# Expert results scaled per slot and added to the output by scattering transfers, in a graph transformer layer

## The chip, the cores and the metric

The kernel runs on one core of a Trainium2 chip. The metric is the device time of one execution in microseconds; of the kernel before there are three runs, with a median of 1598.75 (1598.35 to 1600.05). One further execution was profiled; all rows below are from it.

## The reference, cut to what matters

1250 tokens of width 1024 go through a layer norm, a graph convolution and a linear attention, both added to the input. The change is in the last stage, a mixture of 8 experts of which each token takes the best 2:

```python
x = x + _L0_gnn_ref(xn, edge_index, ...) + _L0_mix_ref(xn[None], ...)[0]
x = x + _L0_ffn_ref(_layernorm(x, axis=-1)[None], ...)[0]

def _L0_ffn_ref(x, gate_w, gate_b, expert_w, expert_b):
    logits = jnp.einsum('bsd,ed->bse', x, gate_w) + gate_b
    topv, topi = jax.lax.top_k(logits, K)          # K = 2 of E = 8
    keep = jax.nn.one_hot(topi, E).sum(axis=-2)
    gate_score = jax.nn.softmax(jnp.where(keep > 0, logits, -jnp.inf), axis=-1)
    expert_out = jnp.einsum('bsd,edo->bseo', x, expert_w) + expert_b
    return jnp.einsum('bseo,bse->bso', expert_out, gate_score)
```

## The kernel before

Five engines run their own instruction streams, written out by hand, and meet only at semaphores. Graph stage and attention are the first two thirds of the span. Then `x2`, the layer's value ahead of the experts, lies in SBUF as 10 tiles of 128 tokens (the last has 98), and its normalised rows in DRAM as `x2n_half[0]` and `x2n_half[1]`, 512 columns each.

*Routing* (VectorE, L1322 to L1413). For every token the two experts and the two gates. Tokens are counted per expert (two small products on TensorE, L1713), and each pair of token and expert gets a slot. An expert has whole tiles of 128 slots, at least two; here there are 23 tiles in all, of at most `MAXT` = 35. The table from slot to token, `slots`, comes from 20 products of one-hot matrices (`hotr`, `hott`, L1721). The gates `gab` are worked out at L1416 to L1424, behind that. `pos` holds the slot of each token's two results.

*Experts.* A tile T is handled so:
- POOL (`gather_tile`, L803 and L806) gathers the tokens' rows into `xg`, in two halves of 512 columns. Half c of tile T + 1 may come when TensorE has transposed that half of tile T.
- TensorE (`tile`) does for each half h four slabs k of the products (three matmul forms L1745, L1746 and L1748 for both column halves), and behind each half the four transpositions of that half of tile T + 1 (L1731). Behind the second half `prod_done` is signalled.
- ScalarE (L1043) and VectorE (L1380) take the transposed half out of PSUM as a high and a low part, `mth` and `mtl`.
- VectorE (`copy_out`, L1393) adds the expert's bias `ebb` to the products and writes `ybuf`. PSUM holds two tiles of products, `ybuf` one.
- SyncE (`store_tile`, L590) stores `ybuf` to the rows of that tile in `slot_y`, a tensor in DRAM of 35 x 128 rows. `slot_y` was filled with rows of `x` in the attention stage (L527), so that no row of it is undefined.

When the last tile of expert e has its products, SyncE issues the 8 slabs (512 KB each) of expert e + 2's weights (L545), and after the tile's store the bias of e + 1. ScalarE (`high`, L1010) and VectorE (L1408) split each slab of expert e + 1 in a high and a low part: slabs 0 to 3 and 4 to 7 behind the two halves of `prepare` for the next tile. Before, VectorE's `copy_out` of an expert's last tile comes behind all of these.

*The end.* Twenty gathers of POOL (L829), 512 KB each, fetch each token's two results from `slot_y`: ten for the first expert as soon as the experts before the last are stored, ten for the second when everything is stored; the last four of these wait for a buffer. VectorE multiplies each by its gate and adds it to `x2` (L1433), and SyncE stores each tile of `x2` to `out` (L615).

Of the kernel before, what the change touches and what calls it, by code (L numbers as in the profile page):

```python
# [24 lines left out]
FILL = MAXT * P // (KT - 1)  # L25
assert FILL * (KT - 1) == MAXT * P and FILL <= NP
# [29 lines left out]
def gps_layer(nc, x, dst_pairs, src_cols, dst_cols, wg, bg, wq, bq, wk, bk, wv, bv, wo, bo, orf,  # L56
              gate_w, gate_b, expert_w, expert_b, out):
    x2n_half = [nc.dram_tensor(f"x2n_half{c}", [NP, CW], F32, kind="Internal").ap() for c in range(NC)]
    slot_y = nc.dram_tensor("slot_y", [MAXT * P, D], F32, kind="Internal").ap()
# [4 lines left out]
    with ctx:  # L64
# [49 lines left out]
        hott = keep("hott", [P, 2 * TT, MAXT], F32, s1)  # L114
# [103 lines left out]
        pc = ExitStack()  # L218
        gathered = keep("gathered", [P, 2 * KT, D], F32, pc)
        pc.close()  # L220
# [32 lines left out]
        pos = keep("pos", [P, 2, TT], I32)  # L253
        token = keep("token", [P, TT], F32)
# [5 lines left out]
        here = keep("here", [P, NC], I32)  # L260
        gw = keep("gw", [P, KT, E], F32)
# [107 lines left out]
        s_pos = sem("s_pos")  # L369
        slot_hot = sem("slot_hot")  # L370
        slots_filled = sem("slots_filled")
# [12 lines left out]
        y_stored = [sem(f"y_stored{c}") for c in range(NC)]  # L384
        z_stored = [sem(f"z_stored{c}") for c in range(NC)]
        a_gathered = sem("a_gathered")
        b_gathered = [sem(f"b_gathered{i}") for i in range(TT // 2)]
        comb_a = sem("comb_a")
        comb_b = sem("comb_b")
# [59 lines left out]
        def _(sp):  # L449
# [72 lines left out]
            with sp.Fori(1, KT) as j:  # L522
                for i, w in enumerate((wk, wv, wq)):

                    sp.wait_ge(a_w, START + 3 * j + i)
                    sp.dma_start(hraw[:, :, :], w[ds(j, 1)].rearrange("a p k n -> (a p) k n")).then_inc(a_raw, 16)
                sp.dma_start(slot_y[ds((j - 1) * FILL, FILL), :], x[0:FILL, :]).then_inc(slots_filled, 16)  # L527

# [57 lines left out]
            def store_tile(T, e, last):  # L586
                for c in range(NC):

                    sp.wait_ge(y_copied[c], T + 3)
                    sp.dma_start(slot_y[ds(T * P, P), c * CW:(c + 1) * CW],  # L590
                                 ybuf[:, c, :]).then_inc((z_stored if last else y_stored)[c], 16)

            def expert(e, par, last):
                more, begin = tiles(sp, e)
                with sp.Fori(0, more) as i:
                    store_tile(tile_of(begin + i), e, last)
                T = tile_of(begin + more)
                if not (isinstance(e, int) and e >= E - 2):

                    sp.wait_ge(prod_done, T + 1)  # L600
                    load_expert(e + 2, par)
                store_tile(T, e, last)
                if not last:

                    load_bias(e + 1)

            sp.wait_ge(slots_filled, 16 * (KT - 1))
            sp.wait_ge(s_cnti, 1)
            experts(sp, expert)


            for t in range(TT):
                n = LAST if t == TT - 1 else P
                sp.wait_ge(comb_b, t + 1)
                sp.dma_start(out[t * P:t * P + n, :], x2[0:n, t, :]).then_inc(s_out, 16)  # L615
# [4 lines left out]
        def _(pool):  # L620
# [31 lines left out]
            for signal in (rest_taken, rest_over, a_w, t_done, s_done, sq_ready, phi_done, kv_done, aux_done, kv_evac,  # L652
                           mt_trans, *y_stored, *z_stored):
                pool.sem_inc(signal, START)
# [116 lines left out]
            g.iota(token[:, :], [[P, TT]], base=0, channel_multiplier=1,  # L771
# [51 lines left out]
            for c in range(NC):  # L823
                pool.wait_ge(y_stored[c], START + 16 * begin)
                apart(pool)

            def gather_results(t, i, at, done):
                n = LAST if t == TT - 1 else P
                g.indirect_dma_start(gathered[0:n, at, :], None, slot_y[:, :],  # L829
                                     bass.IndirectOffsetOnAxis(ap=pos[0:n, i, t:t + 1], axis=0)).then_inc(done, 16)  # L830

            for t in range(TT):
                gather_results(t, 0, t, a_gathered)

            pool.wait_ge(s_pos, 1)
            for c in range(NC):
                pool.wait_ge(z_stored[c], START + 16 + 16 * more)
                apart(pool)
            for t in range(TT):
                if t >= 6:  # L840

                    pool.wait_ge(comb_b, t - 5)
                gather_results(t, 1, TT + t % 6, b_gathered[t // 2])
# [3 lines left out]
        def _(act):  # L847
# [216 lines left out]
        def _(dve):  # L1064
# [271 lines left out]
            v.tensor_tensor(both[:, :, :], oneh[:, 0], oneh[:, 1], ALU.add).then_inc(s_both, 1)  # L1336
            dve.wait_ge(route_done, 1)
# [19 lines left out]
            v.tensor_copy(pos[:, :, :], posf[:, :, :]).then_inc(s_pos, 1)  # L1357
# [25 lines left out]
            def copy_out(T, e, i, begin, last):  # L1383
                for c in range(NC):
                    dve.wait_ge(prod_done, T + 1)
                    dve.wait_ge(eb_ready, 16 * (e + 1))

                    if last:
                        dve.wait_ge(y_stored[c], START + 16 * begin)
                        dve.wait_ge(z_stored[c], START + 16 * i)  # L1390
                    else:
                        dve.wait_ge(y_stored[c], START + 16 * T)
# [3 lines left out]
            def expert(e, par, last):  # L1396
                more, begin = tiles(dve, e)
                with dve.Fori(0, more) as i:
                    for h in range(2):
                        prepare(begin + i + 1, h)  # L1400
                    copy_out(begin + i, e, i, begin, last)
                for h in range(2):
                    prepare(begin + more + 1, h)
                    if not last:
# [5 lines left out]
                copy_out(begin + more, e, more, begin, last)  # L1410

            dve.wait_ge(route_done, 2)
            v.tensor_copy(slots[:, :], bank(2, MAXT)).then_inc(slots_ready, 1)  # L1413

            dve.wait_ge(s_ge, 1)
            link(v.tensor_scalar(gd[:, 3, :], gd[:, 1, :], 1.0, None, ALU.add))  # L1416
            link(v.reciprocal(gd[:, 2, :], gd[:, 3, :]))
            link(v.tensor_tensor(gd[:, 3, :], gd[:, 1, :], gd[:, 2, :], ALU.mult))
            link(v.tensor_tensor(sel[:, 0, :], one, two, ALU.is_lt))
            link(v.tensor_tensor(sel[:, 1, :], two, one, ALU.is_lt))  # L1420
            for i in range(2):
                link(v.tensor_tensor(gab[:, 1, i, :], sel[:, i, :], gd[:, 2, :], ALU.mult))
                link(v.tensor_tensor(gab[:, 2, i, :], sel[:, 1 - i, :], gd[:, 3, :], ALU.mult))
                link(v.tensor_tensor(gab[:, 0, i, :], gab[:, 1, i, :], gab[:, 2, i, :], ALU.add))  # L1424
# [5 lines left out]

            def combine(t, i, at, done):
                n = LAST if t == TT - 1 else P
                v.scalar_tensor_tensor(out=x2[0:n, t, :], in0=gathered[0:n, at, :], scalar=gab[0:n, 0, i, t:t + 1],  # L1433
                                       in1=x2[0:n, t, :], op0=ALU.mult, op1=ALU.add).then_inc(done, 1)

            dve.wait_ge(a_gathered, 16 * TT)
            for t in range(TT):
                combine(t, 0, t, comb_a)
            for t in range(TT):
                dve.wait_ge(comb_a, t + 1)  # L1440
                dve.wait_ge(b_gathered[t // 2], 32)
                combine(t, 1, TT + t % 6, comb_b)
# [3 lines left out]
        def _(pe):  # L1446
# [272 lines left out]
            for i in range(2 * TT):  # L1719
                n = LAST if i % TT == TT - 1 else P  # L1720
                ins = mm(bank(2, MAXT), hotr[0:n, i, :], hott[0:n, i, :], start=(i == 0), stop=(i == 2 * TT - 1))  # L1721
# [96 lines left out]
```

## Time and profile before

| | us |
|---|---|
| median of 3 runs | 1598.75 |
| the profiled execution | 1597.88 |
| its span | 1596.3 |
| TensorE busy in the span | 1410.3 |
| last products of the experts end | 1550.77 |
| stores of the output, first and last issue | 1573.47, 1592.8 |

The span is the time from the first to the last instruction, and the execution takes 1.6 us more. Times in rows count from the start of the span. "Idle before" in brackets is the time that the engine stood still ahead of a row, and what released it. Matmuls are pipelined and their ends modelled. PEclk is the clock granted to TensorE as a share of full speed: 1.00 is 2.4 GHz, 0.50 is 1.2 GHz. A row with "x4" merges four instructions that follow each other.

### The profile page before, as it was taken

How to read it: one execution, taken by the hardware profiler on the slowest of the kernel's cores; microseconds unless marked ns; L12 is line 12 of the kernel's file. 1: busy time of each engine (PE TensorE's matmuls, PEld its weight loads, DVE VectorE, ACT ScalarE, POOL GpSimd, SP SyncE). 2: the span in 40 equal slices, each digit the busy share in tenths (PEclk: the TensorE clock that was granted, in tenths of full speed). 3: DMA queues.
4: the chain of work that ended last, by engine and by line, in shares of the span. 5: the costliest groups of instructions: out<-in, count | busy, mean ns of one | idle time of the engine just before them, and what ended most of it. 6: DMA issues, size and time to landing. Idle time of an engine off the chain costs nothing.

```text
span 1596.3 us, 26325 instructions
## 1 busy us (share of the span) xinstructions
PE 1410.3 (88%) x8396; PEld 1243.6 (78%) x8460; DVE 763.6 (48%) x1492; ACT 466.1 (29%) x777; POOL 381.6 (24%) x380
## 2 busy tenths in 40 slices
PE   5787778978899999999999999997999499999980
PEld 2465566878889999999999999996888388888870
DVE  8755443414344444444444444445454435444536
ACT  7412132401123333333333333333123023223310
POOL 7421443233230101010101010003134211222133
PEclk9999999988899999999999999998999599999995
DMA  4110111244322020202020202004244326666558
GB/s 151 50 37 17 60 47 70 72 137 123 98 71 87 19 87 17 89 15 90 14 91 14 91 13 79 1 1 134 68 140 146 122 88 232 244 237 219 208 195 289
DMA packets 64532, 158.06 MB, mean 99 GB/s; under 512 B 7978, under 2 KB 28922, under 8 KB 64032
## 3 DMA queue, kind: packets, MB, share of 16 engines
q1 hardware_dynamic: 55200, 127.20, 22.5%
q0 software_dynamic: 9280, 30.17, 5.9%
q8 instruction: 32, 0.52, 0.1%
q14 instruction: 20, 0.16, 0.0%
HBM read 119.98 MB, written 55.71 MB: 110 GB/s over the span
## 4 chain that ended last, share of the span: by engine, by line
PE 76%; DMA 7%; DVE 6%; issue 5%; ACT 2%; POOL 2%; DVEq 2%; SPq 1%; POOLq 0%; ACTq 0%
PE PB L1568 7%; PE PB L1570 7%; PE PB L1569 7%; PE PB L1745 5%; PE PB L1746 5%; PE PB L1748 5%; PE PB L1604 5%; PE PB L1627 4%; PE PB L1470 4%; DMA y_scratch<-xrow 3%; PE PB L1552 2%; PE PB L1553 2%; PE PB L1554 2%; PE PB L1511 2%; PE PB L1512 2%
## 5 line engine op out<-in xcount | busy, mean ns | idle before, releaser
L1568 PE MATMUL PB<-xh,hw 128*128 128x416 f32 (+1 forms) x576 | 204.8, 356 | 0.0
L1570 PE MATMUL PB<-xh,hw 128*128 128x416 f32 (+1 forms) x576 | 203.1, 353 | 0.0
L1569 PE MATMUL PB<-xl,hw 128*128 128x416 f32 (+1 forms) x576 | 202.9, 352 | 0.0
L1745 PE MATMUL PB<-mwh,mth 128*128 128x512 f32 x368 | 149.2, 405 | 1.3 <-issue 1.3
L1470 PE MATMUL PB<-ohs,ohd 128*128 x471 | 106.9, 349 | 48.5 <-DVE ohs L1116 34.5
L1746 PE MATMUL PB<-mwl,mth 128*128 128x512 f32 x368 | 144.7, 393 | 0.0
L703 POOL CAST hw<-hraw 128x1024 fp32r<-128x1024 f32 x24 | 24.9, 1038 | 457.6 <-PE PB L1570 456.3
L1470 PEld LDWEIGHTS PB<-ohs,ohd 128*128 x534 | 52.0, 98 | 102.4 <-issue 84.6
L1748 PE MATMUL PB<-mwh,mtl 128*128 128x512 f32 x368 | 114.0, 391 | 0.0
L1114 DVE TENSOR_SCALAR ohd<-iota,dc 128x128 f16 x178 | 56.1, 315 | 114.5 <-PE PB L1470 103.3
L1569 PEld LDWEIGHTS PB<-xl,hw 128*128 128x128 f32 x576 | 108.7, 189 | 1.3
L1568 PEld LDWEIGHTS PB<-xh,hw 128*128 128x128 f32 x576 | 108.6, 189 | 1.3 <-issue 0.2
L1570 PEld LDWEIGHTS PB<-xh,hw 128*128 128x128 f32 x576 | 108.6, 189 | 1.2
L1539 PE MATMUL PB<-hh,AT 128*128 128x256 f32 x400 | 103.7, 298 | 5.9 <-DVE hr L1130 5.8
L1116 DVE TENSOR_SCALAR ohs<-iota,sc 128x1280 f16 x178 | 106.3, 597 | 0.0
L1540 PE MATMUL PB<-hr,AT 128*128 128x256 f32 x400 | 102.2, 294 | 0.0
L1043 ACT ACTIVATE mth<-PB 128x512 fp32r<-128x512 f32 x48 | 28.8, 599 | 231.3 <-PE PB L1731 215.6
L1380 DVE TENSOR_TENSOR mtl<-PB,mth 128x512 fp32r<-128x512 f32 x48 | 33.0, 688 | 131.0 <-ACT mth L1043 126.9
L1511 PE MATMUL PB<-wqh,xh 128*128 128x256 f32 x320 | 91.7, 286 | 3.2 <-DVE xl L1123 1.7
L955 ACT ACTIVATE qf<-PB,biasT 128x416 f32<-128x416 f32 (+1 forms) x48 | 29.2, 609 | 214.5 <-PE PB L1570 167.3
L1512 PE MATMUL PB<-wql,xh 128*128 128x256 f32 x320 | 90.5, 283 | 0.0
L1513 PE MATMUL PB<-wqh,xl 128*128 128x256 f32 x320 | 90.5, 283 | 0.0
(260 smaller groups left out, 3138.6 us busy)
## 6 DMA issues: line engine op xcount, KB each, us to landing
mraw<-expert_w SPq DMA_DIRECT2D x64, 512.0 KB, 5.2
slot_y<-x SPq DMA_DIRECT2D x7, 2560.0 KB, 11.6
slot_y<-ybuf SPq DMA_DIRECT2D x46, 256.0 KB, 3.3
count_rests<-ATf POOLq DMA_DIRECT2D x9, 640.0 KB, 3.3
xrow<-x SPq DMA_DIRECT2D x40, 128.0 KB, 2.4
y_scratch<-xrow SPq DMA_DIRECT2D x40, 128.0 KB, 2.4
yrow<-y_scratch SPq DMA_DIRECT2D x20, 256.0 KB, 2.9
x2n_half<-xhat SPq DMA_DIRECT2D x20, 256.0 KB, 2.5
```

The lines of the kernel that those rows point to most:

```text
L1116: v.tensor_scalar(ohs[:, ds(2 * side + p, 1), :].rearrange("p a n -> p (a n)"), iota[:, :], sc[:, ds(col, 1)], None, ALU.is_equal).then_in ...
L1470: ins = mm(PB[:, 1536 * s + c0:1536 * s + c0 + n], ohd[:, ds(2 * side + p, 1), :].rearrange("p a n -> p (a n)"), ohs[:, ds(2 * side + p, 1 ...
L1511: mm(o, xh[:, k, at], wqh[q % 2][:, k, :], start=(k == 0), stop=False)
L1512: mm(o, xh[:, k, at], wql[q % 2][:, k, :], start=False, stop=False)
L1539: mm(o, AT[:, b, at], hh[:, q % 2, b, :], start=(b == 0), stop=False)
L1540: ins = mm(o, AT[:, b, at], hr[:, q % 2, b, :], start=False, stop=(b == TT - 1))
L1568: mm(bank(i, n), hw[:, wi, 0, k, :], xh[:, k, c0:c0 + n], start=(k == 0), stop=False)
L1569: mm(bank(i, n), hw[:, wi, 0, k, :], xl[:, k, c0:c0 + n], start=False, stop=False)
L1570: ins = mm(bank(i, n), hw[:, wi, 1, k, :], xh[:, k, c0:c0 + n], start=False, stop=(k == KT - 1))
L1745: mm(y[c], mth[:, k, :], mwh[par][:, k, c * CW:(c + 1) * CW], start=(k == 0), stop=False)
L1746: mm(y[c], mth[:, k, :], mwl[par][:, k, c * CW:(c + 1) * CW], start=False, stop=False)
L1748: ins = mm(y[c], mtl[:, k, :], mwh[par][:, k, c * CW:(c + 1) * CW], start=False, stop=(k == KT - 1))
```

## The change

`slot_y`, its fills and stores, the twenty gathers, `pos` and the combination are gone. The output rows get `x2` first, by ten stores that SyncE issues directly after the load of expert 1. Each slot's gate and output row come out of the routing products: `hott` has two values per slot, the token and the gate, 70 columns instead of 35, so the gates are worked out earlier, ahead of the wait for the counts. Empty slots get row 4096, which the transfer leaves out as out of bounds. ScalarE multiplies `ybuf` by the gates of its slots (`scale`), and POOL adds the tile's 128 rows to `out` with one indirect transfer that adds (`add_tile`), waits until it has landed, and signals `y_free`, for which VectorE's next `copy_out` waits. The tile that doesn't exist behind the last one is no longer prepared by ScalarE and VectorE.

```diff
-    slot_y = nc.dram_tensor("slot_y", [MAXT * P, D], F32, kind="Internal").ap()
@@ SyncE
-                sp.dma_start(slot_y[ds((j - 1) * FILL, FILL), :], x[0:FILL, :]).then_inc(slots_filled, 16)
...
             load_expert(1, 1)
+            for t in range(TT):
+                n = LAST if t == TT - 1 else P
+                sp.dma_start(out[t * P:t * P + n, :], x2[0:n, t, :]).then_inc(s_out, 16)
...
-                store_tile(T, e, last)
                 if not last:
 
+                    for c in range(NC):
+                        sp.wait_ge(y_copied[c], T + 3)
                     load_bias(e + 1)
@@ POOL
+            def add_tile(T):
+
+                pool.wait_ge(y_scaled, NC * (T + 1))
+                apart(pool)
+                g.tensor_copy(there[:, :], target[:, ds(T, 1)]).then_inc(there_ready, 1)
+                pool.wait_ge(there_ready, T + 1)
+                apart(pool)
+                g.indirect_dma_start(out[:, :], bass.IndirectOffsetOnAxis(ap=there[:, 0:1], axis=0),
+                                     ybuf[:, :, :].rearrange("p c n -> p (c n)"), None, bounds_check=N - 1,
+                                     oob_is_err=False, compute_op=ALU.add).then_inc(y_added, 16)
+                pool.wait_ge(y_added, 16 * (T + 1))
+                pool.sem_inc(y_free, 1)
+
             more, begin = tiles(pool, E - 1)
-            with pool.Fori(0, begin + more + 1) as T:
+            gather_tile(1)
+            pool.wait_ge(s_out, 16 * TT)
+            pool.wait_ge(targets_ready, 1)
+            with pool.Fori(1, begin + more + 1) as T:
                 gather_tile(tile_of(T + 1))
+                add_tile(tile_of(T - 1))
+            add_tile(tile_of(begin + more))
@@ ScalarE
+            def scale(T):
+                for c in range(NC):
+                    act.wait_ge(y_copied[c], T + 3)
+                    apart(act)
+                    a.mul(ybuf[:, c, :], ybuf[:, c, :], gate[:, ds(T, 1)]).then_inc(y_scaled, 1)
+
...
                     for h in range(2):
                         prepare(begin + i + 1, h)
-                for h in range(2):
-                    prepare(begin + more + 1, h)
-                    if not last:
+                    scale(tile_of(begin + i))
+                if not last:
+                    for h in range(2):
+                        prepare(begin + more + 1, h)
+                        if h == 1:
+                            scale(tile_of(begin + more))
                         for k in range(4 * h, 4 * h + 4):
                             high(e + 1, k, 1 - par)
+                else:
+                    scale(tile_of(begin + more))
@@ VectorE (the same order of copy_out in its expert)
-            for i in range(2):
-                v.tensor_tensor(hott[:, i * TT:(i + 1) * TT, :], hota[:, i * TT:(i + 1) * TT, :],
-                                token[:, :].rearrange("p (t a) -> p t a", a=1).broadcast_to([P, TT, MAXT]),
-                                ALU.mult).then_inc(slot_hot, 1)
+            for i, value in enumerate((token[:, :], gab[:, 0, :, :].rearrange("p i t -> p (i t)"))):
+                v.tensor_tensor(hott[:, :, i, :], hota[:, :, :], along(value, MAXT), ALU.mult).then_inc(slot_hot, 1)
...
-                        dve.wait_ge(y_stored[c], START + 16 * T)
+                    dve.wait_ge(y_free, T + START)
```

POOL's instructions in the expert stage, before: the loop over tiles (two gathers), and the gathers of the results behind it.

```order
L803 ISA [waits mt_trans]
L803 COPY here<-slots 128x1
L804 REGISTER_ALU
L806 DMA xg<-x2n_half,here 128x512 [waits here_ready]
L803 COPY here<-slots 128x1 [waits mt_trans]
L804 REGISTER_ALU
L806 DMA xg<-x2n_half,here 128x512 [waits here_ready]
```

And now; `there` holds the output rows of the tile, `target` those of all tiles.

```order
L785 COPY here<-slots 128x1 [waits mt_trans]
L786 REGISTER_ALU
L788 DMA xg<-x2n_half,here 128x512 [waits here_ready]
L803 REGISTER_ALU
L805 ISA [waits y_scaled]
L805 COPY there<-target 128x1
L808 DMA out<-ybuf,there 1250x1024 [waits there_ready]
L811 REGISTER_ALU
L818 ISA [waits y_added]
```

Behind the second gather the loop has gained a copy and a transfer, with waits for the scaled rows and for the landing, ahead of the next tile's gathers.

ScalarE at the end of an expert's last tile, before: the second half's preparation and four casts of weights.

```order
L1043 ACTIVATE mth<-PB 128x512 [waits mt_trans]
L1010 ACTIVATE mwh<-mraw 128x1024 [waits mw_raw4]
L1010 ACTIVATE mwh<-mraw 128x1024 [waits mw_raw5]
L1010 ACTIVATE mwh<-mraw 128x1024 [waits mw_raw6]
L1010 ACTIVATE mwh<-mraw 128x1024 [waits mw_raw7]
```

And now:

```order
L1021 ACTIVATE mth<-PB 128x512 [waits mt_trans]
L1026 REGISTER_ALU
L1028 ISA [waits y_copied0]
L1028 ACTIVATE ybuf<-ybuf,gate 128x512
L1028 ACTIVATE ybuf<-ybuf,gate 128x512 [waits y_copied1]
L988 ACTIVATE mwh<-mraw 128x1024 [waits mw_raw4]
L988 ACTIVATE mwh<-mraw 128x1024 [waits mw_raw5]
```

Two scalings, each behind VectorE's copy of its half, now stand ahead of the casts.

## Rows read from the trace of the kernel before

**Rows 1.** The page: busy us, share of the span, instructions.

```profile
PE 1410.3 (88%) x8396; PEld 1243.6 (78%) x8460; DVE 763.6 (48%) x1492; ACT 466.1 (29%) x777; POOL 381.6 (24%) x380
```

**Rows 2.** Engines by stretch: its us, busy us (count), PEclk, DMA share, GB/s.

```profile
1450.00:1500.00 50.00, 50.00 (x239) 41.35 (x237) 29.01 (x33) 20.56 (x25) 10.54 (x18) 1.00 0.70 263
...
1550.00:1596.30 46.30, 1.21 (x8) 0.80 (x6) 26.26 (x23) 0.60 (x1) 18.27 (x14) 0.54 0.84 307
```

**Rows 3.** Timeline of the tail: start, us, engine, line, work, idle before and releaser.

```profile
1550.15 0.62 PE L1748 MATMUL PB<-mwh,mtl 128*128 128x512 f32 x2
...
1556.37 0.60 ACT L1043 ACTIVATE mth<-PB 128x512 fp32r<-128x512 f32 x1 [10.37 <-remote]
...
1557.60 1.28 DVE L1393 TENSOR_TENSOR ybuf<-PB,ebb 128x512 f32<-128x512 f32 x2
...
1560.01 19.42 DVE L1433 SCALAR_TENSOR_TENSOR x<-gathered,gab,x 128x1024 f32<-128x1024 f32 x16 [1.13 <-DMA gathered<-slot_y,pos]
...
1562.08 1.26 POOL L829 DMA_INDIRECT gathered<-slot_y,pos  x1 [8.17 <-DMA slot_y<-ybuf]
...
1573.72 6.52 POOL L829 DMA_INDIRECT gathered<-slot_y,pos  x1 [4.18 <-DVE x L1433]
```

**Rows 4.** Timeline, an ordinary tile of the expert stage.

```profile
1503.19 0.60 PE L1731 MATMUL PB<-ident,xg 128*128 128x128 f32 x4
...
1505.15 1.28 DVE L1393 TENSOR_TENSOR ybuf<-PB,ebb 128x512 f32<-128x512 f32 x2
```

**Rows 5.** Timeline, an expert's last tile (products end at 1515.2).

```profile
1515.05 0.60 PE L1731 MATMUL PB<-ident,xg 128*128 128x128 f32 x4
...
1516.26 3.89 ACT L1010 ACTIVATE mwh<-mraw 128x1024 fp32r<-128x1024 f32 x4
...
1516.88 0.97 POOL L806 DMA_INDIRECT xg<-x2n_half,here  x1 [0.79 <-POOL here L803]
...
1517.35 4.63 DVE L1408 TENSOR_TENSOR mwl<-mraw,mwh 128x1024 fp32r<-128x1024 f32 x4 [0.26 <-ACT mwh L1010]
...
1520.97 0.60 PE L1731 MATMUL PB<-ident,xg 128*128 128x128 f32 x4
```

**Rows 6.** Landing times: the gathers of slot_y (min/median/max).

```profile
DMA to landing us min/median/max: 4.8/6.0/11.8
```

**Rows 7.** GB/s in 40 slices of 1240 to 1269.

```profile
GB/s 0 164 418 373 384 384 379 407 429 412 424 424 401 424 401 322 40 0 0 0 0 0 0 0 0 0 0 0 0 0 0 0 0 0 0 0 0 0 0 0
```

**Rows 8.** Chain that ended last: start, us, what (the expert stage's first gather).

```profile
1268.92 3.57 DMA xg<-x2n_half,here
```

**Rows 9.** Issues and landings in the load of a later expert: stores, 1320 to 1331; slabs.

```profile
slot_y<-ybuf SPq DMA_DIRECT2D x2, 256.0 KB, 9.5
...
L545 SPq DMA_DIRECT2D mraw<-expert_w x8: 311/346/733, 1313.9 to 1317.7; - x8
...
DMA to landing us min/median/max: 3.4/6.3/9.2
```

**Rows 10.** Timeline of routing, VectorE and TensorE.

```profile
1246.70 0.24 DVE L1339 COPY tot<-PB 128x80 f32<-128x80 f32 x1 [1.97 <-PE PB L1714]
...
1257.34 0.88 DVE L1372 TENSOR_TENSOR hota<-nums,posa 128x700 f32<-128x700 f32 x1
...
1258.26 0.96 DVE L1374 TENSOR_TENSOR hott<-hota,token 128x350 f32<-128x350 f32 x2
...
1259.27 8.75 PE L1721 MATMUL PB<-hott,hotr 128*128 128x35 f32 x40 [12.60 <-DVE hott L1374]
...
1268.16 0.16 DVE L1416 TENSOR_SCALAR gd<-gd 128x10 f32<-128x10 f32 x1
...
1270.26 0.17 DVE L1424 TENSOR_TENSOR gab<-gab 128x10 f32<-128x10 f32 x1
```

**Rows 11.** Engines by stretch, two stretches with waits, early.

```profile
163.00:165.60 2.60, 1.07 (x10) 1.06 (x10) 0.00 (x0) 1.38 (x4) 2.60 (x4) 1.00 0.45 132
...
236.20:243.10 6.90, 4.04 (x12) 1.89 (x14) 4.68 (x11) 0.00 (x0) 2.15 (x2) 0.51 0.26 95
```

More of the change, by code:

```diff
@@ L24 @@
 MAXT = (2 * N + 2 * (P - 1)) // P + 1 + 2 * (E - 2) + 1
-FILL = MAXT * P // (KT - 1)
-assert FILL * (KT - 1) == MAXT * P and FILL <= NP
+FAR = 4096
 CHUNKS = ((0, 512), (512, 512), (1024, NP - 1024))
@@ L113, in gps_layer @@
         hota = keep("hota", [P, 2 * TT, MAXT], F32, s1)
-        hott = keep("hott", [P, 2 * TT, MAXT], F32, s1)
+        hott = keep("hott", [P, 2 * TT, 2, MAXT], F32, s1)
         s1.close()
@@ L215, in gps_layer @@
         pr.close()
-        pc = ExitStack()
-        gathered = keep("gathered", [P, 2 * KT, D], F32, pc)
-        pc.close()
         mwh0 = keep("mwh0", [P, KT, D], F32R)
@@ L252, in gps_layer @@
         posf = keep("posf", [P, 2, TT], F32)
-        pos = keep("pos", [P, 2, TT], I32)
-        token = keep("token", [P, TT], F32)
+        token = keep("token", [P, 2 * TT], F32)
         posa = keep("posa", [P, 2 * TT], F32)
@@ L260, in gps_layer @@
         here = keep("here", [P, NC], I32)
+        target = keep("target", [P, MAXT], I32)
+        there = keep("there", [P, 1], I32)
+        gate = keep("gate", [P, MAXT], F32)
         gw = keep("gw", [P, KT, E], F32)
@@ L368, in gps_layer @@
         s_cnti = sem("s_cnti")
-        s_pos = sem("s_pos")
         slot_hot = sem("slot_hot")
-        slots_filled = sem("slots_filled")
         slots_ready = sem("slots_ready")
@@ L383, in gps_layer @@
         y_copied = [sem(f"y_copied{c}") for c in range(NC)]
[L384 to L389, printed above, removed]
+        targets_ready = sem("targets_ready")
+        y_scaled = sem("y_scaled")
+        there_ready = sem("there_ready")
+        y_added = sem("y_added")
+        y_free = sem("y_free")
         s_out = sem("s_out")
@@ L584, in _ @@
             load_expert(1, 1)
[L586 to L591, printed above, removed]
+            for t in range(TT):
+                n = LAST if t == TT - 1 else P
+                sp.dma_start(out[t * P:t * P + n, :], x2[0:n, t, :]).then_inc(s_out, 16)
             def expert(e, par, last):
                 more, begin = tiles(sp, e)
-                with sp.Fori(0, more) as i:
-                    store_tile(tile_of(begin + i), e, last)
                 T = tile_of(begin + more)
@@ L601, in expert @@
                     load_expert(e + 2, par)
-                store_tile(T, e, last)
                 if not last:
+                    for c in range(NC):
+                        sp.wait_ge(y_copied[c], T + 3)
                     load_bias(e + 1)
-            sp.wait_ge(slots_filled, 16 * (KT - 1))
             sp.wait_ge(s_cnti, 1)
             experts(sp, expert)
[L612 to L615, printed above, removed]
             sp.wait_ge(s_out, 16 * TT)
@@ L652, in _ @@
             for signal in (rest_taken, rest_over, a_w, t_done, s_done, sq_ready, phi_done, kv_done, aux_done, kv_evac,
-                           mt_trans, *y_stored, *z_stored):
+                           mt_trans, y_free):
                 pool.sem_inc(signal, START)
@@ L770, in _ @@
                    allow_small_or_imprecise_dtypes=True).then_inc(s_route_const, 1)
-            g.iota(token[:, :], [[P, TT]], base=0, channel_multiplier=1,
+            g.iota(token[:, :], [[0, 2], [P, TT]], base=-FAR, channel_multiplier=1,
                    allow_small_or_imprecise_dtypes=True).then_inc(s_route_const, 1)
@@ L818, in _ @@
                                      bass.IndirectOffsetOnAxis(ap=here[:, c:c + 1], axis=0)).then_inc(xg_ready[c], 16)
+            def add_tile(T):
[9 more added lines that the diff above has]
+                pool.sem_inc(y_free, 1)
             more, begin = tiles(pool, E - 1)
-            with pool.Fori(0, begin + more + 1) as T:
+            gather_tile(1)
+            pool.wait_ge(s_out, 16 * TT)
+            pool.wait_ge(targets_ready, 1)
+            with pool.Fori(1, begin + more + 1) as T:
                 gather_tile(tile_of(T + 1))
[L823 to L843, printed above, removed]
+                add_tile(tile_of(T - 1))
+            add_tile(tile_of(begin + more))
         @block.scalar
@@ L1336, in _ @@
             v.tensor_tensor(both[:, :, :], oneh[:, 0], oneh[:, 1], ALU.add).then_inc(s_both, 1)
+            dve.wait_ge(s_ge, 1)
+            link(v.tensor_scalar(gd[:, 3, :], gd[:, 1, :], 1.0, None, ALU.add))
+            link(v.reciprocal(gd[:, 2, :], gd[:, 3, :]))
+            link(v.tensor_tensor(gd[:, 3, :], gd[:, 1, :], gd[:, 2, :], ALU.mult))
+            link(v.tensor_tensor(sel[:, 0, :], one, two, ALU.is_lt))
+            link(v.tensor_tensor(sel[:, 1, :], two, one, ALU.is_lt))
+            for i in range(2):
+                link(v.tensor_tensor(gab[:, 1, i, :], sel[:, i, :], gd[:, 2, :], ALU.mult))
+                link(v.tensor_tensor(gab[:, 2, i, :], sel[:, 1 - i, :], gd[:, 3, :], ALU.mult))
+                link(v.tensor_tensor(gab[:, 0, i, :], gab[:, 1, i, :], gab[:, 2, i, :], ALU.add))
             dve.wait_ge(route_done, 1)
@@ L1356, in _ @@
                 link(v.tensor_reduce(posf[:, i, :], both[:, :, :], AX.X, ALU.add))
-            v.tensor_copy(pos[:, :, :], posf[:, :, :]).then_inc(s_pos, 1)
             flat = posf[:, :, :].rearrange("p i t -> p (i t)")
@@ L1381, in prepare, with copy_out @@
                                 mth[:, 4 * h:4 * h + 4, :].bitcast(F32), ALU.subtract).then_inc(mt_low, 1)
-            def copy_out(T, e, i, begin, last):
+            def copy_out(T, e):
                 for c in range(NC):
@@ L1386, in copy_out @@
                     dve.wait_ge(eb_ready, 16 * (e + 1))
[L1388 to L1391, printed above, removed]
-                        dve.wait_ge(y_stored[c], START + 16 * T)
+                    dve.wait_ge(y_free, T + START)
                     v.tensor_tensor(ybuf[:, c, :], PB[:, ds((T & 1) * D + c * CW, CW)], ebb[:, c * CW:(c + 1) * CW],
@@ L1400, in expert @@
                         prepare(begin + i + 1, h)
[L1401 to L1404, printed above, removed]
+                    copy_out(begin + i, e)
+                if not last:
+                    for h in range(2):
+                        prepare(begin + more + 1, h)
+                        if h == 1:
+                            copy_out(begin + more, e)
                         for k in range(4 * h, 4 * h + 4):
@@ L1409, in expert @@
                                             mwh[1 - par][:, k, :].bitcast(F32), ALU.subtract).then_inc(mw_ready, 1)
-                copy_out(begin + more, e, more, begin, last)
+                else:
+                    copy_out(begin + more, e)
             dve.wait_ge(route_done, 2)
[L1413 to L1424, printed above, removed]
+            found = bank(2, 2 * MAXT)
+            v.tensor_scalar(slots[:, :], found[:, 0:MAXT], float(FAR), float(N - 1), ALU.add, ALU.min).then_inc(slots_ready, 1)
+            v.tensor_copy(gate[:, :], found[:, MAXT:2 * MAXT])
+            v.tensor_scalar(target[:, :], found[:, 0:MAXT], float(FAR), None, ALU.add).then_inc(targets_ready, 1)
             dve.wait_ge(s_cnti, 1)
@@ L1428, in _ @@
             experts(dve, expert)
[L1431 to L1442, printed above, removed]
         @block.tensor
@@ L1720, in _ @@
                 n = LAST if i % TT == TT - 1 else P
-                ins = mm(bank(2, MAXT), hotr[0:n, i, :], hott[0:n, i, :], start=(i == 0), stop=(i == 2 * TT - 1))
+                ins = mm(bank(2, 2 * MAXT), hotr[0:n, i, :], hott[0:n, i, :, :].rearrange("p a s -> p (a s)"),
+                         start=(i == 0), stop=(i == 2 * TT - 1))
             ins.then_inc(route_done, 1)
```

## The prediction

> **What bounds the kernel now.** I began with the busy shares of the page: TensorE is busy for 1410.3 of 1596.3 us [rows 1], so only what stops it can move the time much, or what runs when it has ended. The table of engines by stretch shows both states: 50.00 of 50 us with the clock at its full level in the middle of the expert stage, and 1.21 of 46.3 us in the last stretch, with the DMA engines 84% busy [rows 2]. The reader is to see a tail of transfers behind the last product. The timeline of that tail gives its parts [rows 3]: the last products end at 1550.77; ScalarE's last preparation starts only at 1556.37; the last copy from PSUM runs from 1557.60 to 1558.88; the second gathers start at 1562.08; the seventh of them takes 6.52 us from 1573.72; the span ends at 1596.3. So 45.5 us lie behind the products. The execution took 1597.88 us, 1.6 more than its span, and 0.9 less than the 1598.75 median of the runs.
>
> Call P the moment at which a tile's products end. TensorE goes tile by tile in 11.85 us (the transpositions that follow a tile's products start at 1503.19 and, one tile later, 1515.05, some 0.17 ahead of the products' modelled end [rows 4, 5]) and asks for half a gathered tile twice in each: at P, and again at P + 5.75 (1520.97 against 1515.2) [rows 5].
>
> **The tail: -33.** Gone are the store, twenty gathers, twenty combinations and the ten stores of the output, which had to follow each other. What stays behind the last P: copying from PSUM ends 3.1 us after P in an ordinary tile (1503.36 to 1506.43; two halves in 1.28) [rows 4], but in the last expert the preparation of a tile that doesn't exist is gone from VectorE and ScalarE, so I take 1.5. Then one scale of the second half, 0.6 (a ScalarE operation of 1024 columns costs 3.89/4 = 0.97; the half width is nearer 0.6) [rows 5], 0.1 between engines, and POOL's copy of the indices, 0.2, its 0.79 of waiting and the launch [rows 5], so that the add starts near P + 3.4. A gather of a whole tile, 512 KB, lands 4.8 to 11.8 us after its start, median 6.0 [rows 6]; I take 6.0 for the add, which the trace doesn't have, and 0.4 for the end: 9.8. That is 45.5 - 9.8 = 35.7 less. One part is uncertain: ScalarE waited 10.37 us for a signal that I can't place ("remote"), 5.2 us past the last transposition at 1551.2. The first ten gathers were on the DMA engines just then, and the new kernel has none there; but nothing excludes that the same delay follows the last product again. Both ends are kept, -35.7 and -30.3, and I take the middle, -33.
>
> In its own sentences: the Trainium skill (Collectives: The Full Stack, "Why ReduceScatter is half of AllGather") says that an add in a DMA engine costs because each chunk needs two source reads. No row here shows an add. By it, with 512 KB at the 400 GB/s of [rows 7], the estimate would be 4.8 + 1.3 = 6.1, not 4.8, and in a busy queue 1.3 more as well; with the cheap end instead of it the sum below would lose some 7 us.
>
> **The new chain through POOL: +17.** The order shows that in POOL's loop an add with two waits now stands between the gathers: POOL stands still until the add has landed, and behind it in its queue are both gathers of the tile after next. For a tile with end P: copied at P + 3.1, scaled at + 3.75 (0.6 for the half that is last), index copy, 0.79 of waiting: the add starts at P + 5.2. With L for its landing, POOL is free at P + 5.2 + L, the gather's signal, index copy and wait take 1.2 (0.2 + 0.2 + 0.79) [rows 5], and a gather of 256 KB lands 3.6 us after its start [rows 8]. TensorE asks for it at P + 11.85 + 5.75 = 17.6. So there is no stall while L is below 17.6 - 5.2 - 1.2 - 3.6 = 7.6. In a quiet queue L = 6.0 fits, and so does the 4.8 of the quickest gather; the 11.8 of the slowest doesn't, and I keep it as the upper end.
>
> Six times the queue isn't quiet. When an expert's last tile ends, SyncE issues 8 slabs of 512 KB for the expert after next, from 1313.9 to 1317.7 [rows 9]; P was 1313.7, 17 tiles of 11.85 ahead of 1515.2. In that time a store of only 256 KB landed after 9.5 us [rows 9]. The add starts 5.2 us into this. I take 9.5 for it, between 6.3 (the median slab of that load) and the 11.8 of the slowest gather. Then the gather starts at P + 15.9, lands at about + 20.4 (4.5, since the load isn't quite over), and TensorE waits 2.8. A second delay, of the gather that is now issued at P + 0.6, inside the load, where it was 5 us before it, costs 0.6 + 6.3 - 5.75, about 1 us. It isn't added: it puts TensorE's next request off by the same 1 us, so both delays together are 2.8. VectorE's next copy waits for the add too, until P + 14.7 instead of P + 13.6; TensorE wants that buffer only at P + 23.7, so it costs nothing. Six loads (experts 2 to 7): 6 x 2.8 = 17, bounds 0 (L of 6.3 there) and 6 x 5.5 = 33.
>
> **Expert switches: +1.** ScalarE's two scales now stand between the second half's preparation and the last four of the weight casts, and VectorE's copy ahead of the four subtractions. Before, the first of the four casts began at P + 1.06 [rows 5]; now at P + 3.95, so the first subtraction is ready at P + 6.2 and TensorE wants it at 6.1. From then on it uses a slab in some 1.4 us (11.85 / 8, less the transposing), and the subtractions deliver one each 1.16 (4.63 / 4) [rows 5]: 0.1 to 0.2 us at 7 switches, 1 us; if scaling costs as much as 1024 columns, 0.97, it is 0.9 each, 6 us.
>
> **Routing: +1.5.** Eleven small gate operations (1268.16 to 1270.43, 2.27 us, hidden by the first gather) move ahead of the counts, where VectorE idled 1.97 us for TensorE until 1246.70: +0.3. The two 350-element products of 0.96 us together become two of 700 like the 0.88 us comparison: +0.8. The position cast of 0.17, half hidden, goes: -0.1. The forty matmuls (8.75 us) take 70 columns instead of 35 at the lower clock level; 35 columns at 1.2 GHz are 0.03 us of the 0.219 that one costs, so the width is not what it pays for [rows 10]. I take +0.5, between 0 and +1.2 (40 x 0.03).
>
> **At nothing.** The ten output stores (5.1 MB) are issued right after the load of expert 1. The row of GB/s from 1240 to 1269, in slices of 0.73 us, shows that load over near 1252 and nothing until the first gather; at the 400 GB/s seen there 5.1 MB take 13 us, to 1265. POOL's wait for all ten, ahead of its loop, is then over when it comes. If they ran past 1269 the first gather would pay the excess, up to 4 us [rows 7]. The seven fills of slot_y in the attention stage and 46 slot stores only free a queue that nobody waits for; expert 1's bias rows come no later than they did.
>
> **Sum.** 1597.9 - 33 + 17 + 1 + 1.5 = 1584.4, and 0.9 more for the median: **1585 us**.
>
> **Rivals.** (a) The add is as quick as a store also during loads, 6.3 or less: no stall at all, 1597.9 + 2.5 - 33 + 0.9 = 1568. For it: engines drain two queues side by side, and POOL's add isn't behind the slabs in SyncE's queue. Against it: the gathers' own maximum of 11.8.
> (b) The other side: an add into memory is slow by itself, at L = 9.2 quiet. Then every tile's gather is late by 1.6 us, 16 x 1.6 = 26, and the six loaded ones, at 12.7, by 6: 36. That is 1568 + 62, less some overlap: 1620, slower than before. It decides from about L = 8.2 on (16 x 0.6 + 6 x 4 = 33). For it: nothing in this trace reads and writes back the same rows; against: 6.0 leaves 1.6 us of room.
> (c) The waits bring TensorE down to 1.2 GHz. A stretch of 6.9 us in which it was busy 4.04, so idle 2.9, ran at 0.51; one of 2.6 us with 1.5 idle stayed at 1.00 [rows 11]. Six falls of some 7 to 10 us at half speed cost 4 to 5 us each: 1585 + 27 = 1612.
> (d) POOL can't write the add's descriptors while VectorE subtracts with both inputs in SBUF: the launch of 6.52 us ended 0.8 us after a run of such operations [rows 3]. At a switch the four subtractions (4.63 us) now lie where the add is launched, so it would start 3.4 us later, 7 times: 1585 + 20 = 1605. Against it: the launch at 1516.88 kept 0.97 us though a subtraction began at 1517.35 [rows 5]. The Trainium skill (SBUF — State Buffer, "Who interferes with whom") names such a lock only for operations in a two-port mode or for POOL's reads; by that rule (d) would cost nothing.
>
> **Chances.** Forecast 0.45 (its own range 1573 to 1595), (a) 0.25, (b) 0.2, (c) 0.06, (d) 0.04. Less than 0.2% (3.2 us) can't be told from no change. Nearly all of the forecast and (a) is faster: 0.70; same 0.04; slower 0.26. The range leaves out the best of (a) and the upper half of (b): 1564 to 1618.
>
> **What would show it.** The stretch between the last product and the end: 10 to 15 us instead of 45.5. TensorE's idle time in the expert stage before transpositions (reason: a gather): six waits of 2 to 4 us, none in quiet tiles; idle in every tile says (b), and none says (a). POOL's longest wait should be for its own add. The clock column must stay at 1.00 from the second tile on, else (c). An add launch far above 1 us says (d). I am wrong if an add takes over 8 us in a quiet tile, or if the stall comes through the copies waiting for the buffer and not through the gathers.

## The result: 0.6% slower, not 0.9% faster

Both kernels ran seven times in turn on one chip: 1598.35 us before (1596.13 to 1600.05), 1608.55 after (1602.06 to 1613.13), ratio 1.0057, 95% interval 1.0043 to 1.0071. The forecast was 1585, its range 1564 to 1618: the time lies inside the range, but above before's where it was forecast below. The profiled execution took 1608.55, 10.7 more than before's 1597.88. Laid beside each other, the two executions part at three places:

| stretch | before | after | difference | forecast |
|---|---|---|---|---|
| start to the expert stage's first product | 1276.27 | 1279.71 | +3.4 | +1.5 |
| expert stage, first product to last | 274.5 | 309.8 | +35.3 | +18 |
| tail, last product to the end | 45.5 | 17.5 | -28.0 | -33 |

The row of busy engines answers to [rows 1]: the same 8396 matmuls now keep TensorE busy 12 us longer.

```profile
PE 1422.6 (89%) x8396; PEld 1250.1 (78%) x8460; DVE 739.0 (46%) x1471; ACT 495.4 (31%) x821; POOL 403.3 (25%) x406
```

The engines by stretch (stretch, its us, then PE, PEld, DVE, ACT and POOL busy with their counts, PEclk, DMA share, GB/s), for the expert stage and the tail of after:

```profile
1279.70:1589.50 309.80, 286.74 (x1286) 233.09 (x1287) 121.99 (x145) 108.72 (x144) 95.72 (x133) 0.95 0.58 165
1589.50:1607.00 17.50, 0.42 (x4) 0.18 (x2) 1.29 (x2) 1.33 (x2) 1.78 (x2) 0.64 0.09 12
```

and for the stage of before:

```profile
1276.30:1550.80 274.50, 274.50 (x1286) 226.58 (x1287) 121.70 (x146) 80.03 (x101) 59.42 (x97) 0.99 0.56 199
```

This is the view to read first. The count of matmuls is the same, so the 35.3 us split in two: 309.8 - 286.7 = 23.1 in which TensorE stood idle, and 286.7 - 274.5 = 12.2 in which the same products took longer. The clock column, 0.95 for 0.99, says why: part of the stage ran at the lower of the two levels, 1.2 GHz for 2.4.

**The idle part.** The waits of after (engine and line, what it waited for, total us, times, longest):

```profile
POOL here L785 <- DMA out<-ybuf,there: 67.9, 9, 9.1
PE PB L1706 <- DMA xg<-x2n_half,here: 27.3, 10, 4.5
```

POOL waits for its own add, and TensorE for gathered rows: 4.5 of the 27.3 fall before the stage, six waits in the stage make 21.6 (3.93, 3.68, 2.88, 4.05, 3.80, 3.22), one at each load of an expert's weights, as forecast. But how each comes about differs. The timeline of POOL, with ScalarE's scale, around the first of them (start, us, engine, line, work, idle before and its releaser); the transpositions behind the tile before last of that expert started at 1305.0 and those behind the last at 1316.8 (the prediction's P is 0.17 later, 1317.0), and SyncE issued the eight slabs right behind P:

```profile
1307.83 1.34 ACT L1028 ACTIVATE ybuf<-ybuf,gate 128x512 f32<-128x512 f32 x2 [1.52 <-DVE ybuf L1385]
...
1308.99 0.97 POOL L788 DMA_INDIRECT xg<-x2n_half,here  x1 [0.79 <-POOL here L785]
...
1311.09 1.63 POOL L808 DMA_INDIRECT out<-ybuf,there  x1 [0.93 <-POOL there L805]
1318.03 0.18 POOL L785 COPY here<-slots 128x1 int32 x1 [5.31 <-PE PB L1706]
1319.00 1.00 POOL L788 DMA_INDIRECT xg<-x2n_half,here  x1 [0.79 <-POOL here L785]
...
1320.98 0.97 POOL L788 DMA_INDIRECT xg<-x2n_half,here  x1 [0.79 <-POOL here L785]
1321.96 0.19 POOL L805 COPY there<-target 128x1 int32 x1
1323.08 1.65 POOL L808 DMA_INDIRECT out<-ybuf,there  x1 [0.92 <-POOL there L805]
1333.71 0.18 POOL L785 COPY here<-slots 128x1 int32 x1 [8.98 <-DMA out<-ybuf,there]
```

```profile
1326.84 0.63 PE L1706 MATMUL PB<-ident,xg 128*128 128x128 f32 x4 [3.93 <-DMA xg<-x2n_half,here]
```

The rows of the add of 1311.09 were scaled at 1309.17, but POOL was still at the two gathers ahead of it in its loop, until 1309.96. The add landed after 6.2 us, at 1317.3, 0.3 behind P. (The releaser named for the copy at 1318.03 is a transposition that ended a moment before; a wait for two things is put down to one.) The gather behind it started at 1319.00, 1.8 us into the load, and landed in 7.7 us instead of 3.6 [rows 8]. TensorE had asked for it at 1322.9. The add inside the load, launched at 1323.08, did hold POOL up to 1333.7, about as forecast, but by then TensorE was 3.9 us late itself and its next rows came in time.

**The slower part.** At five of the six waits (all but the 2.88) the granted clock fell to the lower level for 3.4 us or 6.8 us; the falls began between 2.0 us before the wait's end and 1.4 us behind it. Right behind the first:

```profile
1327.00:1333.00 6.00, 6.00 (x22) 4.81 (x22) 0.69 (x1) 0.60 (x1) 0.00 (x0) 0.72 1.04 324
```

TensorE is busy without a gap here, but does 22 matmul records in 6 us where the stage at full clock has 28 (1286 in 274.5).

**The tail.** VectorE, ScalarE and POOL, which answer to [rows 3]:

```profile
1589.70 1.29 DVE L1385 TENSOR_TENSOR ybuf<-PB,ebb 128x512 f32<-128x512 f32 x2 [9.49 <-PE PB L1723]
1590.59 1.33 ACT L1028 ACTIVATE ybuf<-ybuf,gate 128x512 f32<-128x512 f32 x2 [9.44 <-DVE ybuf L1385]
1592.17 0.19 POOL L805 COPY there<-target 128x1 int32 x1 [7.35 <-ACT ybuf L1028]
1593.27 1.59 POOL L808 DMA_INDIRECT out<-ybuf,there  x1 [0.91 <-POOL there L805]
```

The add starts 3.8 us behind the last product and lands at 1599.35, after 6.1. Then the program isn't over: POOL's record has one more instruction, a drain that closes its program, from 1599.43 to 1606.78 (the views above don't count it as work, the trace has it). Before had it too, 16.65 us long from 1577.08 to 1593.7, beside the last combinations and stores of the output, where it hid.

### The profile page after: what moved, and what is told of

Its sections match the earlier page's. It is cut to its first block, busy times and chain, and to the rows that moved or that the text cites. A ratio compares the mean times of both kernels' runs of the same rounds, so it can differ in the third digit from the quotient of the medians.

```text
span 1607.0 us, 26378 instructions
## 1 busy us (share of the span) xinstructions
PE 1422.6 (89%) x8396; PEld 1250.1 (78%) x8460; DVE 739.0 (46%) x1471; ACT 495.4 (31%) x821; POOL 403.3 (25%) x406
## 3 DMA queue, kind: packets, MB, share of 16 engines
q1 hardware_dynamic: 48016, 96.79, 17.6%
## 4 chain that ended last, share of the span: by engine, by line
PE 68%; DMA 13%; DVE 6%; issue 6%; ACT 2%; POOL 1%; DVEq 1%; SPq 1%; POOLq 0%; ACTq 0%
PE PB L1542 7%; PE PB L1544 7%; PE PB L1543 7%; PE PB L1578 5%; PE PB L1601 4%; PE PB L1444 4%; DMA y_scratch<-xrow 4%; PE PB L1720 3%; PE PB L1721 3%; PE PB L1723 3%; DMA out<-ybuf,there 3%; DMA xg<-x2n_half,here 2%; PE PB L1526 2%; PE PB L1528 2%; PE PB L1527 2%
## 5 line engine op out<-in xcount | busy, mean ns | idle before, releaser
L1720 PE MATMUL PB<-mwh,mth 128*128 128x512 f32 x368 | 152.9, 415 | 1.4 <-issue 1.3
L1721 PE MATMUL PB<-mwl,mth 128*128 128x512 f32 x368 | 148.2, 403 | 0.0
L1513 PEld LDWEIGHTS PB<-hh,AT 128*128 128x128 f32 x400 | 80.8, 202 | 8.1 <-DVE hr L1119 6.9
```

The lines of the kernel that those rows point to most:

```text
L1513: mm(o, AT[:, b, at], hh[:, q % 2, b, :], start=(b == 0), stop=False)
L1720: mm(y[c], mth[:, k, :], mwh[par][:, k, c * CW:(c + 1) * CW], start=(k == 0), stop=False)
L1721: mm(y[c], mth[:, k, :], mwl[par][:, k, c * CW:(c + 1) * CW], start=False, stop=False)
```

## Experiments

All against the kernel before on the same chip: 1602.52 us there for the first four, 1601.64 for the last three. Stage, idle and tail are of the one profiled execution of each; kernel 4, whose expert stage is the changed kernel's, has a stage 1.7 us longer than that one, so differences of that size say nothing.

| kernel | us | ratio (95%) | stage | TensorE idle in it | tail |
|---|---|---|---|---|---|
| 1 no_pool_wait | 1585.31 | 0.9898 (0.9882-0.9915) | 287.2 | 10.3 | 17.6 |
| 2 load_after_gather | 1631.43 | 1.0186 (1.0169-1.0203) | 333.3 | 41.7 | 17.6 |
| 3 plain_scatter | 1583.35 | 0.9884 (0.9866-0.9902) | 288.7 | 9.3 | 14.7 |
| 4 last_add_awaited_by_sync | 1605.64 | 1.0023 (1.0010-1.0037) | 311.5 | 24.2 | 14.5 |
| 5 no_pool_wait_at_all | 1585.09 | 0.9876 (0.9841-0.9911) | 287.2 | 9.5 | 14.2 |
| 6 early_bias | 1570.46 | 0.9802 (0.9769-0.9834) | 275.5 | 0 | 13.9 |
| 7 early_bias_pool_waits | 1606.18 | 1.0024 (1.0004-1.0044) | 306.2 | 21.5 | 17.6 |

**1. POOL no longer waits for the add.** VectorE, which reuses the buffer, waits for it directly (an added small DMA, `first`, starts the count at 16). `ybuf` is one buffer, so two adds are still never on their way together.

```
-                pool.wait_ge(y_added, 16 * (T + 1))     # in add_tile
-                pool.sem_inc(y_free, 1)
-                    dve.wait_ge(y_free, T + START)      # in copy_out
+                    dve.wait_ge(y_added, 16 * (T + 1))
```

> Only change to the new kernel: POOL no longer waits for its add to land; VectorE's next copy waits for that landing itself (a small transfer ahead of the loop gives the count its start). POOL's one wait is at the very end. Theory A (POOL standing still behind its add brings the next gather into the weight load, where it lands in 8 us instead of 4, and the idle time brings the clock down): the 27 us of waits for gathers go, PEclk stays 1.00 after the second tile, and with 8 to 11 us of lower clock gone too the time is 1608 - 37 = about 1572. Rival B (the adds' own traffic, double reads, delays gathers and loads): the waits stay, 1600 to 1608.

The six waits of 3 to 4 us and every fall of the clock in the stage are gone: POOL's wait for the landing is what cost. The time is 13 us above the 1572 expected, because the stage is still 12.7 us over before's, with eight waits of 0.3 to 1.8 (the stage by engines, and waits):

```profile
1281.90:1569.10 287.20, 276.93 (x1286) 226.13 (x1287) 122.39 (x145) 106.86 (x144) 108.93 (x133) 0.99 0.60 178
```

```profile
DVE ybuf L1385 <- DMA ebb<-expert_b: 29.0, 6, 6.4
DVE ybuf L1385 <- DMA out<-ybuf,there: 23.5, 11, 4.8
...
PE PB L1706 <- DMA xg<-x2n_half,here: 12.9, 8, 4.5
```

**2. The load goes out only when the next gather has landed.** If the late gather were all, that should free it from the load.

```
                     sp.wait_ge(prod_done, T + 1)
+                    sp.wait_ge(xg_ready[0], 16 * (T + 3))
                     load_expert(e + 2, par)
```

> The new kernel, but SyncE issues the 8 slabs of a later expert only when the gather of the first half of the tile after next has landed (about 5 us later). Theory A: six waits of 3 to 4 us vanish, and as no add lands sooner, at most the waits that I had forecast for the add inside the load (2.8 each) come in their place: 1575 to 1595. Rival B, or the load simply shifting its pressure to the second half's gather: within 5 us of 1608.

Neither reading holds: slower, with six waits of 4.9 to 7.3 us. POOL's waits in this kernel:

```profile
POOL here L786 <- DMA out<-ybuf,there: 121.5, 18, 10.1
DVE ybuf L1386 <- DMA ebb<-expert_b: 58.7, 6, 11.0
PE PB L1707 <- DMA xg<-x2n_half,here: 46.3, 13, 7.3
```

and its timeline around a load:

```profile
1326.80 1.65 POOL L809 DMA_INDIRECT out<-ybuf,there  x1 [0.92 <-POOL there L806]
1338.03 0.19 POOL L786 COPY here<-slots 128x1 int32 x1 [9.58 <-DMA out<-ybuf,there]
1339.01 1.00 POOL L789 DMA_INDIRECT xg<-x2n_half,here  x1 [0.79 <-POOL here L786]
```

The first gather is in time now. The add of 1326.80 meets the load instead, which now starts at 1325.4. It holds POOL idle for 9.6 us, and TensorE waits 6.8 us for the gather behind it. (VectorE waits up to 11.0 us for the new bias rows, which are loaded behind the slabs, but this add belongs to the old expert.) That is the chain that the prediction had priced, at 2.8 us a load; in the changed kernel the earlier stall covers it. So there are two delays, and the wait on POOL is behind both: moving the load only trades one for the other.

**3. A write in place of the add** (the output then holds the last writer's rows, not the sum).

```
-                                     oob_is_err=False, compute_op=ALU.add).then_inc(y_added, 16)
+                                     oob_is_err=False).then_inc(y_added, 16)
```

> The new kernel with the scattering transfers writing rows instead of adding to them (the output is then not the sum). Tells what the add costs beside a write: if it needs a second read, a landing of 5 instead of 6.2 us in quiet tiles and a launch of 1.0 instead of 1.6; POOL is free 1.8 us sooner, the gather starts before the load, and the six waits shrink by half: about 1595. If landing and launch stay, the time stays at 1608.

The landings of the scattering transfer, first with the add (the changed kernel), then as a write:

```profile
DMA to landing us min/median/max: 6.1/6.3/10.3
```

```profile
DMA to landing us min/median/max: 3.2/3.4/8.6
```

The launch took 1.02 us for 1.63. With POOL still waiting for every landing, 2.9 us less from an add's start to its landing, the launch included, brought the first gather 0.5 us ahead of the tile's end (1316.73, for a transposition at 1317.17) instead of 2.2 behind it, and so ahead of the load: 9.3 us idle instead of 23.1, one fall of the clock, 12 us less than the 1595 expected. So what POOL's wait costs hangs on where it puts the gather, ahead of the load or inside it. What is left is mostly the chain that the prediction had priced: the write of 1322.69 holds POOL until 1332.0, and TensorE waits 1.4 us for the gather behind it.

**4. SyncE waits for the last add, not POOL.** This is about the closing drain alone.

```
-            add_tile(tile_of(begin + more))
+            add_tile(tile_of(begin + more), True)        # True: without POOL's wait
...                                                       # at SyncE's end:
+            sp.wait_ge(y_added, 16 * (begin + more + 1))
```

> The new kernel, but the last add's landing is awaited by SyncE and not by POOL, so that POOL's closing drain (7.3 us after the last landing) can begin when the add is launched. Theory C (the drain is a fixed work of POOL's own, 7.4 us from its start): it ends 4.5 us sooner, 1604. Rival D (it begins to count at the landing): unchanged, 1608.

3.0 us less of tail, between the two readings; the time itself, on another chip, can't tell. The drain now starts at the launch of the add, at 1597.37, and takes 10.3 us instead of 7.3. It neither costs a fixed time from its start nor a fixed time from the landing; about half of its 7.3 us can lie beside the transfer. In the four kernels in which it began before POOL's last transfer had landed (before, 4, 5, 6) it ended 3.6 to 3.7 us behind that landing.

**5. Both: no wait on POOL at all** (1 and 4 together).

> As the kernel in which VectorE alone waits for the add, and SyncE instead of POOL waits for the last one, so that POOL's closing drain can start as soon as the last add is launched. The stage should not change (287 us, waits of 10 us). If the drain costs 7 us from the landing whoever waits, the tail stays at 17.6 and the time at 1585; if it runs partly beside the add's flight, as in the experiment that did only this (tail 14.5 instead of 17.5), the time is 1582.

The tail fell from 17.6 to 14.2, as the second reading said. The time, 1585.09, can't be told from that of 1: its runs reach from 1579.95 to 1585.94, and its profile has one wait of 2.69 us with a fall of the clock at its end.

**6. The bias an expert ahead,** on top of 5: two buffers. The bias rows are still loaded behind the eight slabs, but they are those of the expert after next, so nobody waits for them yet. (One more wait of SyncE, ahead of a load, keeps a slab's count of landings in order; it wasn't tried by itself.)

```
+        ebbs = (ebb[:, :], x2[:, 0, :])
...
                     load_expert(e + 2, par)
-                if not last:
                     for c in range(NC):
                         sp.wait_ge(y_copied[c], T + 3)
-                    load_bias(e + 1)
+                    load_bias(e + 2, par)
```

> The kernel of e5_no_pool_wait_at_all, and the bias rows of an expert in two buffers, fetched an expert ahead instead of behind the eight slabs at the switch. Theory: the 10.2 us of waits that are left there come from the late bias (first copy of an expert waits until it lands), which delays copy, scale, add, and so the next gather, queued behind the add on POOL. Then VectorE waits for no bias any more, TensorE's waits in the expert stage fall to 2 us or less, the stage to about 277 and the time to 1572. Rival: gathers are slow because adds and loads share the engines; then the waits stay near 10 us and the time near 1582.

The expert stage and the tail:

```profile
1276.60:1552.10 275.50, 275.46 (x1286) 226.01 (x1287) 122.33 (x145) 107.76 (x144) 107.86 (x133) 0.99 0.64 183
1552.10:1566.00 13.90, 0.45 (x5) 0.21 (x2) 1.29 (x2) 1.33 (x2) 1.80 (x2) 0.64 0.11 15
```

No idle time, no slower clock, 275.5 us for before's 274.5. The late bias was the cause of the rest: with no wait for landing left, POOL still handles add and gathers in order, and at each switch the add waited for the scale, the scale for the copy, and the copy for the bias. (VectorE's splits of the weights stand behind that copy too, and TensorE waited for them once, 1.8 us, in kernel 1.) In kernel 5, where kernel 6 has no wait for bias rows at all:

```profile
DVE ybuf L1387 <- DMA ebb<-expert_b: 27.9, 6, 6.1
...
DVE ybuf L1387 <- DMA out<-ybuf,there: 21.5, 11, 4.4
```

Before had that wait as well (28.9 us, 6 times), at no cost: its slot stores went out through SyncE's queue, with no gather behind them. This kernel beats before by 2.0% (1.7% to 2.3%) and the changed kernel by some 2.5%, by the two ratios to before (0.9802 and 1.0057). Of the 18.4 us between the profiled executions of 5 and 6, the stage has 11.8; 6.4 had arisen before the routing, where the two programs are alike, and aren't the bias's.

**7. The early bias with POOL's wait kept.**

> The changed kernel with the early bias alone; POOL still waits for every add. Theory: its six waits of 3 to 4 us come from POOL standing still until the add of the expert's last but one tile has landed, so that the gather goes out inside the load; the bias has no part in them: six waits as before, 1605 to 1609. What it can take away is the add in the load itself, later by the bias. Rival: the late bias is what delays everything at a switch also here: the waits fall by 10 us or more and the time below 1597.

Nothing gained that can be told from the changed kernel's own time (1.0024 here, 1.0057 there, on different chips). TensorE's and POOL's waits are much the changed kernel's:

```profile
POOL here L788 <- DMA out<-ybuf,there: 58.2, 8, 9.1
...
PE PB L1709 <- DMA xg<-x2n_half,here: 26.3, 9, 4.5
```

Six waits of 3.1 to 3.8 us. So the landing comes first and the bias second: either edit alone leaves a limit, 1606 with only the bias, 1585 with only the wait gone, 1570 with both.

## Why the prediction was wrong

By its own steps, against the profiled execution (forecast 1584.4, measured 1608.55: 24.2 too little). The steps that failed are the second delay, left out of the sum, the clock behind the waits, left to a rival, and the end of the tail.

- **Tail, -33, measured -28.0 (5.0 of the 24.2).** Its mechanism was right: copy 0.2 us behind the products, add at + 3.8 (forecast 3.4), landing 6.1 (6.0). The 5.4-us delay of a signal, kept as a bound, doesn't occur. What failed is "0.4 for the end", which measured 7.6; the 2.7 us that the middle of the two bounds held for the signal hid a third of that by luck. The 0.4 was read off a program whose last work is VectorE's and SyncE's, while the new one ends on POOL, whose drain takes 7.3 us. Experiments 4 and 5 showed how much of the drain can be had back, 3.0 to 3.4 us.
- **The chain through POOL, +17, measured 23.1 idle (6.1).** The count (six), the place (the loads) and the engine (TensorE waiting for a gather) were right, and the add's landing too, 6.3 quiet for 6.0, up to 10.3 loaded for 9.5. The step that failed is "a second delay ... about 1 us. It isn't added". It was the only one that TensorE felt. In that sum, 0.6 + 6.3 - 5.75, the gather started at P + 0.6; it started at P + 2.0. The add began 5.9 behind its tile's end instead of 5.2, because the sum followed the rows through VectorE and ScalarE and left out that POOL itself was busy with the two gathers ahead of the add; it landed in 6.2, not 6.0; and POOL needed 1.7 from landing to the next start instead of 1.2. And the gather landed in 7.7, not in the 6.3 of a median slab: 2.0 + 7.7 - 5.9 = 3.8, of the 3.93 that the row shows. Of two delays that hide each other the larger counts, and the one called smaller had been priced from optimistic terms. Experiment 2 shows the other one when the first is gone, at 4.9 to 7.3 us a load.
- **The clock, rival (c), at 0.06, measured 11.2 (with the 1.0 of the switches 12.2).** This was the worst judgement. The forecast's own waits were of 2.8 us, and the very row it cited had 2.9 idle with the clock at 0.51 [rows 11]. The falls follow from the forecast's waits and are no rival to them, though not every such wait brings one: 2.88 us had none here, 2.69 in experiment 5 had one. The price per fall was too high, some 2 us in five falls for 4 to 5 in six. So (c)'s 1612 is near the time partly by luck: too dear in the clock, too cheap in the waits and the tail.
- **Switches, +1: right.** Experiment 6, with no wait and no fall, has a stage 1.0 us longer than before's. Its clock rose to the full level 2.9 us into the stage, before's 4.4 and the changed kernel's 4.1, so the switches themselves cost nearer 1.7, and the falls nearer 10.6 than 11.2. A scale took 0.72 us (0.6 assumed).
- **Routing, +1.5, measured 0.9;** the other 2.5 us of the first stretch arose ahead of it, where the two programs are alike (TensorE's routing product starts at 1262.82 for 1259.27, with 2.6 of it from before the routing). That part differs from one execution to the next: the changed kernel and the seven experiments reach their first product at 1276.6 to 1283.0. The product of 70 columns took 8.81 us for 8.75 [rows 10]: the width costs nothing, as forecast.
- **At nothing: right.** The ten output stores (issued 1246.2 to 1252.5) kept the DMA engines at 406 GB/s up to 1267 and were over before the first gather of 1272.5.
- **Rivals.** (a) is out: the add needs up to 10.3 us in a load. (b) is out: the median of all 23 is 6.3. (d) is out: no launch of the 23 took over 1.95 us.

With a first delay of 3.9 instead of 2.8, six times, 5 falls at 2.2 and 7.3 of drain the same sum gives 1597.9 - 28 + 23.4 + 11 + 1 + 1.5 = 1607.

## What to carry to other kernels

A transfer that an engine waits for also delays whatever stands behind it in that engine's queue; let the engine that reuses the buffer wait, and the queue go on. When a wait is added to an in-order queue, list everything that the queued work now depends on, down to a bias row that was harmlessly late. If a forecast contains idle times of TensorE, price the clock behind them in the same sum, and look at which engine the program ends on.

## What the runs showed of the hardware

- An accumulating scatter of 128 rows of 4 KB landed in 6.3 us (median) where the same scatter as a write took 3.4, and its launch on POOL took 1.63 us for 1.02.
- POOL's closing drain lasted 7.0 to 7.3 us when POOL had already waited for its last transfer, and 9.8 to 10.3 when it hadn't, 3 us sooner over in all. Begun before the last landing, it ended 3.6 to 3.7 us behind it. Why it takes so long stays open.
- A gather of 256 KB started 1.8 us into a load of eight slabs took 7.7 us for 3.6 in a quiet queue.
- Waits of TensorE of 3 to 4 us each cost nearly half as much again through the clock: 23.1 idle and at most 11.2 slower in after, 21.5 and 9.2 in experiment 7 (306.2 - 275.5 - 21.5).
